# First convolution tap of three channel tiles on ScalarE instead of VectorE in a Mamba scan kernel

## The reference, cut to what matters

```python
def step(h, inp):
    d_t, B_t, C_t, u_t = inp
    h = h * jnp.exp(d_t[..., None] * A) + (d_t * u_t)[..., None] * B_t[:, None, :]
    y = jnp.einsum('bcn,bn->bc', h, C_t)
    return (h, y)
...
def _mamba_layer(x, Wi, cw, cb, Wx, Wdt, bdt, Alog, Dp, Wo):
    xz = jnp.einsum('bld,ed->ble', x, Wi)
    xin, z = jnp.split(xz, 2, axis=-1)
    xin = _silu(_causal_conv(xin, cw, cb))
    x_dbl = jnp.einsum('blc,ec->ble', xin, Wx)
    dt_raw = x_dbl[..., :DT_RANK]
    Bm = x_dbl[..., DT_RANK:DT_RANK + D_STATE]
    Cm = x_dbl[..., DT_RANK + D_STATE:]
    delta = jax.nn.softplus(jnp.einsum('blr,cr->blc', dt_raw, Wdt) + bdt)
    A = -jnp.exp(Alog)
    y = _selective_scan(delta, Bm, Cm, xin, A, Dp)
    y = y * _silu(z)
    return jnp.einsum('blc,dc->bld', y, Wo)
for i in range(DEPTH):
    x = x + _mamba_layer(x, W_in[i], conv_w[i], ...)
```

## Time and profile before

| what | value |
|---|---|
| median of 3 runs | 7742.98 us (7742.54 to 7743.24) |
| profiled execution, its own time | 7743.71 us |
| span of its trace | 7742.0 us, mean granted clock 0.987 |
| PE busy | 6941.3 us |
| DVE busy | 6668.0 us |
| ACT busy | 6422.9 us |
| POOL busy | 5929.2 us |

### The profile page before, as it was taken

The page is one execution under the profiler, slowest core; times in us unless marked ns, Lnnn a source line. Parts: engine busy times, 40 slices in busy tenths (PEclk is TensorE's granted clock), DMA queues, the critical chain, the costliest instruction groups (busy, mean ns, idle before and its releaser), DMA issues. The chain is left out here.

```text
span 7742.0 us, 143629 instructions
## 1 busy us (share of the span) xinstructions
PE 6941.3 (90%) x39999; PEld 4801.8 (62%) x39999; DVE 6668.0 (86%) x6510; ACT 6422.9 (83%) x10314; POOL 5929.2 (77%) x4917
## 2 busy tenths in 40 slices
PE   6979999999999999999999999999999999999997
PEld 4646666666666666666666666666666666666665
DVE  3259988988998899889889988988998898889888
ACT  1258888888888888888888888888888888888887
POOL 2148887888888888888888887888888788888875
PEclk9989999999999999999999999999999999999998
DMA  4111111111111111111111111111111111111112
GB/s 161 34 42 40 40 39 47 43 39 40 42 45 44 39 39 48 42 40 39 40 46 44 40 38 41 45 42 39 39 48 42 39 40 41 45 43 39 40 39 91
DMA packets 222613, 352.40 MB, mean 46 GB/s; under 512 B 43856, under 2 KB 78448, under 8 KB 221712
## 3 DMA queue, kind: packets, MB, share of 16 engines
q1 hardware_dynamic: 218048, 332.70, 14.6%
q0 software_dynamic: 3792, 10.38, 0.4%
HBM read 325.00 MB, written 17.98 MB: 44 GB/s over the span
## 5 line engine op out<-in xcount | busy, mean ns | idle before, releaser
L884 POOL TENSOR_TENSOR drive<-du,brep 128x512 f32<-128x512 f32 x4096 | 5505.9, 1374 | 708.3 <-DVE du L1127 385.6
L916 ACT ACTIVATE ps_d<-delta,cur 128x512 f32<-128x512 f32 x4096 | 2869.9, 701 | 373.9 <-DVE state L1077 354.8
L923 ACT ACTIVATE prod<-ps_r,cT 128x512 f32<-128x512 f32 x4096 | 2837.1, 693 | 245.4 <-PE ps_r L1231 243.9
L1231 PE MATMUL ps_r<-ident,state 128*128 128x128 f32 x16384 | 2564.0, 280 | 297.1 <-ACT prod L923 158.3
L1077 DVE TENSOR_TENSOR_SCAN state<-ps_d,carry,drive 128x512 f32<-128x512 f32 x2048 | 2517.7, 1266 | 260.6 <-ACT ps_d L916 258.5
L1077 DVE TENSOR_TENSOR_SCAN state<-ps_d,drive 128x512 f32<-128x512 f32 x2048 | 2396.8, 1206 | 245.6 <-ACT ps_d L916 233.0
L1238 PE MATMUL ps_y<-ident,prod 128*128 128x128 f32 x16384 | 2481.9, 276 | 25.9 <-ACT prod L923 25.9
L1238 PEld LDWEIGHTS ps_y<-ident,prod 128*128 128x128 f32 x16384 | 1938.9, 142 | 666.8 <-issue 499.4
L1231 PEld LDWEIGHTS ps_r<-ident,state 128*128 128x128 f32 x16384 | 1851.3, 142 | 729.9 <-ACT prod L923 462.5
L1278 PE MATMUL ps_r<-xm,w_inz_sb 128*128 128x512 f32 x1024 | 507.4, 618 | 81.6 <-ACT prod L923 81.6
L1270 PE MATMUL ps_r<-xm,w_inx_sb 128*128 128x512 f32 x1024 | 509.1, 620 | 21.9 <-ACT prod L923 14.2
(11 more groups left out here) (144 smaller groups left out, 4647.3 us busy)
## 6 DMA issues: line engine op xcount, KB each, us to landing
brep<-bc_dram SPq DMA_DIRECT2D x1024, 256.0 KB, 3.2
w_sb<-w SPq DMA_DIRECT2D x8, 1024.0 KB
w_all<-w SPq DMA_DIRECT2D x8, 1024.0 KB, 11.4
xb<-xs_dram SPq DMA_DIRECT2D x39, 128.5 KB, 2.0
w_all<-x SPq DMA_DIRECT2D x4, 1024.0 KB, 9.1
w_inx_sb<-w_in SPq DMA_DIRECT2D x8, 512.0 KB, 4.1
w_inz_sb<-w_in SPq DMA_DIRECT2D x8, 512.0 KB, 4.5
w_out_sb<-w_out SPq DMA_DIRECT2D x8, 512.0 KB, 4.2
```

Source lines behind the costliest of these rows:

```text
L884: nc.gpsimd.tensor_tensor(drive[:, k % DRIVE, :], du[:, j, :], brep[:, n % BREP, :], ALU.mult).then_inc(drive_set, 1)
L916: nc.scalar.activation(ps_d[:, k % 2, :], delta[h][:, j, :], ACT.Exp, scale=cur[h][:, a:a + 1]).then_inc(decay_set, 1)
L923: nc.scalar.activation(prod[:, t, :], ps_r[:, item_place(U, h, kind, item), :], ACT.Copy, scale=cT[(h + 1) % 2 if item[1] == "prev" else h ...
L1231: last = nc.tensor.transpose(out[:, j * P:(j + 1) * P], state[STATE_IN[n]][:, j, t * P:(t + 1) * P], ident[:])
```

## The change

ScalarE makes, right behind the copy of tile 0, 1 or 2, a second activation from the same place of the ring: Identity with the weight of the last tap as scale and the convolution bias as bias, written to `xc`. Only this second activation counts up `ring_act`. VectorE leaves the first tap out; its second tap now waits for that count. The two waits of tile 0 (its weights are loaded, the SiLU of the unit before has read `xc`) move to ScalarE. `conv_step` counts two instead of three steps per tile. A table `DECAYS` is introduced for the order of the exponentials; with `BOOST_AT` and `REST_AT` empty it gives the order that was there.

```diff
+BOOST_AT, REST_AT = [], []
...
+LEAD = 2
...
+DECAYS, at = {}, LEAD
+for n, j in [(n, j) for n in range(STATES) for j in range(CB)]:
+    count = 1 + BOOST_AT.count((n, j)) - REST_AT.count((n, j))
+    DECAYS[n, j] = list(range(at, at + count))
+    at += count
...
             def copy_x(U, h, kind, F, j):
+                at = item_place(U, h, kind, f"X{j}")
                 act.wait_ge(ring_ready, item_ready(U, kind, f"X{j}"))
                 act.wait_ge(halo_set, F + 1)
-                nc.scalar.activation(xpad[:, j, TAPS - 1:], ps_r[:, item_place(U, h, kind, f"X{j}"), :], ACT.Copy).then_inc(ring_act, 1)
+                copied = nc.scalar.activation(xpad[:, j, TAPS - 1:], ps_r[:, at, :], ACT.Copy)
+                if j in DVE_CONV:
+                    if j == DVE_CONV[0]:
+                        act.wait_ge(taps_in[h], loads_of(F, h))
+                        if not is_first(F):
+                            act.wait_ge(u_set, F)
+                    copied = nc.scalar.activation(xc[:, j, :], ps_r[:, at, :], ACT.Identity, scale=taps[h][:, j * TAPS + TAPS - 1:j * TAPS + TAPS],
+                                                  bias=taps[h][:, COL_CB + j:COL_CB + j + 1])
+                copied.then_inc(ring_act, 1)
...
-                if k == 0:
+                if k == 1:
                     dve.wait_ge(ring_act, copied)
-                    if j == DVE_CONV[0]:
-                        dve.wait_ge(taps_in[h], loads_of(G, h))
-                        if not is_first(G):
-                            dve.wait_ge(u_set, G)
-                    step = nc.vector.tensor_scalar(xc[:, j, :], xpad[:, j, tap:tap + T], w,
-                                                   taps[h][:, COL_CB + j:COL_CB + j + 1], ALU.mult, ALU.add)
                 else:
-                    dve.wait_ge(conv_step, (TAPS - 1) * (CV * G + DVE_CONV.index(j)) + k)
-                    step = nc.vector.scalar_tensor_tensor(xc[:, j, :], xpad[:, j, tap:tap + T], w, xc[:, j, :], ALU.mult, ALU.add)
+                    dve.wait_ge(conv_step, (TAPS - 2) * (CV * G + DVE_CONV.index(j)) + k - 1)
+                step = nc.vector.scalar_tensor_tensor(xc[:, j, :], xpad[:, j, tap:tap + T], w, xc[:, j, :], ALU.mult, ALU.add)
...
-                    if (n, j) == CONV_AT[i]:
+                    if (n, j) == CONV_AT[i] and i % TAPS:
```

More of the change, by code:

```diff
@@ L1019, in unit @@
                     for t in range(TC):
[L1020 to L1024, removed]
+                        for k in DECAYS[n, t]:
+                            if k < TILES:
+                                exponent(U, h, k)
+                            elif kind != "last":
+                                exponent(U + 1, 1 - h, k - TILES)
                         if (n, t) == SILU_AT:
@@ L1051, in _ @@
                     early(0, 0, "pre1", 1, n, t)
-            exponent(0, 0, 0)
-            exponent(0, 0, 1)
+            for k in range(LEAD):
+                exponent(0, 0, k)
             units(act, unit)
@@ L1162, in late @@
                 for i in range(CV * TAPS):
-                    if (n + STATES, j) == CONV_AT[i]:
+                    if (n + STATES, j) == CONV_AT[i] and i % TAPS:
                         conv(copied, F, hf, DVE_CONV[i // TAPS], i % TAPS)
```

## The result

The changed kernel takes **7863.15 us** (median of 4 runs, 7836.52 to 7904.57) against 7743.11 us for the kernel before beside it: ratio 1.016, 95% interval 1.0114 to 1.0205. It is slower by 120 us, outside the predicted range of 7720 to 7792. The spread is a result too: 68 us between its runs, 2 us between those of the kernel before (6 to 22 us in the larger sets of its runs beside the experiments). The profiled execution took 7871.91 us, its span is 7870.2 us.

What follows compares the result with a forecast made beforehand. No engine was saturated; the bound changes hands, mainly between VectorE and ScalarE. Activations less tap gains cost 46 us over 31 periods, the clock returns 33: +13 us, forecast 7755 us, range 7720 to 7792.

Steps and rivals of the forecast that it cites:

- Tile 0's tap in h = 1: At step (5,1), the second tap ends 0.55 us behind GpSimd's instruction, at 31.89 instead of 32.42; VectorE gains 0.52 us.
- PE's wait at `DT0`: In h = 1, PE's wait for `add_x` shrinks from 1.25 to 0.37 us, so its clock should no longer fall.
- the first rival: PE's granted clock in h = 1 keeps falling behind step (6,2), leaving only the price: 7789 us; chance 0.25.
- The price of the fall: PE's clock fall in h = 1 costs 1.07 us a period, 224.07 against 225.14 us; its absence gains 33 us.
- Scan (11,3): At tile 2, this VectorE scan waits about 0.9 us for ScalarE's exponential instead of 0.25 us.
- tile 0 with the clock: Gains at step (5,1), 0.05 us in h = 0 and 0.52 us in h = 1, plus 33 us from the clock.
- tile 1: At step (9,0), the activation costs 0.06 us in h = 0 and 0.66 us in h = 1, before scan (9,3).
- the 0.66 us in both units at tile 2: At step (11,0), the added activation is exposed in full before scan (11,3), 0.66 us in h = 0 and h = 1.
- the one on the removed tap at (15,1): Tile 2's removed VectorE tap, 0.53 us, gains at most 0.2 us before ScalarE is the bound; taken as 0.
- The rival of the passed-over tap: A second tap is held through one more GpSimd instruction once a period, 1.24 us, 38 us in all: 7793 us; chance 0.08.
- The list of edits at nothing: SiLU wait, weight loads, exponential table, GpSimd's steps, DMAs and PE's ring places were given no cost of their own.
- The third rival: VectorE is the bound: the 0.53 us at (15,1) pass on in both units, giving 7709 us; chance 0.12.

Runs made afterwards that it cites:

- tap at (15,1) put back: Changed kernel with ScalarE's loop at slot 60 and VectorE's first tap of tile 2 done once more at (15,1), same values: 7757.10 us.
- with tiles 0 and 1: Changed kernel with ScalarE's loop at slot 60 and tile 2's first tap left on VectorE as before: 7731.89 us, ratio 0.9989.
- slot 60: Changed kernel with only the start of ScalarE's loop body fixed to the 60th slot of an instruction block: 7800.87 us; the kernel before, so placed: 7745.91 us.
- tile 0 alone: Only tile 0's first tap on ScalarE, tiles 1 and 2 as in the kernel before, ScalarE's loop at slot 60: 7705.67 us, in a second set 7701.64 us.
- slot 8: The kernel before with only ScalarE's loop body moved to the eighth slot of an instruction block: 7841.71 us, ratio 1.0121.
- (1,1): Changed kernel with ScalarE's loop at slot 60 and tile 2's second tap moved from (1,0) one scan later: 7923.94 us, ratio 1.0235.
- (0,3): Changed kernel with ScalarE's loop at slot 60 and tile 2's second tap moved from (1,0) to one scan earlier: 7762.19 us, ratio 1.0027.

## Why the prediction was wrong

**What held.** The new activation takes 0.77 us (forecast about 0.78), and 0.66 us from its start to that of the next instruction, as forecast. Tile 0's tap in h = 1 ends at 3179.25, 0.55 us behind GpSimd's group, as forecast (the group below: 3167.56 + 11.14 = 3178.70), and PE's wait at `DT0` is 0.34 us (forecast 0.37). The clock in h = 1 is 1.00 behind it, against 0.79 in the earlier trace rows; in the loop it falls there in 22 of 30 units before and in none after, so the first rival is out. The price of the fall holds too: the kernel before takes 224.07 us (median) for the 7 periods in which the granted clock stays at 1.00, and 225.19 us for the 23 others. Scan (11,3) waits 0.90 us (forecast about 0.9: 0.25) and scan (9,3) waits for ScalarE.

```profile
3167.56 11.14 POOL L891 TENSOR_TENSOR drive<-du,brep 128x512 f32<-128x512 f32 x9
```

By tiles, in us:

| | forecast | measured |
|---|---|---|
| tile 0 with the clock | -18 - 33 = -51 | -39 and -43 |
| tile 1 | 31 x 0.72 = +22 | +26 to +30 |
| tile 2, tap at (15,1) put back | 31 x 1.32 = +41 | 7757.10 - 7731.89 = +25 |
| sum | +13 | 7757.10 - 7743.82 = +13 |

The terms are off by 4 to 16 us each and cancel, so the agreement of the sums is luck. The largest miss is the 0.66 us in both units at tile 2. Scan (11,3) of h = 0 and h = 1, first with tiles 0 and 1, then with all three and the tap put back (the kernel before waits 0.25 and 0.23 us):

```profile
3060.95 1.22 DVE L1104 TENSOR_TENSOR_SCAN state<-ps_d,drive 128x512 f32<-128x512 f32 x1 [0.62 <-ACT ps_d L934]
...
3173.30 1.28 DVE L1104 TENSOR_TENSOR_SCAN state<-ps_d,carry,drive 128x512 f32<-128x512 f32 x1 [0.23 <-ACT ps_d L934]
```

```profile
3070.80 1.22 DVE L1105 TENSOR_TENSOR_SCAN state<-ps_d,drive 128x512 f32<-128x512 f32 x1 [0.90 <-ACT ps_d L935]
...
3183.65 1.28 DVE L1105 TENSOR_TENSOR_SCAN state<-ps_d,carry,drive 128x512 f32<-128x512 f32 x1 [0.75 <-ACT ps_d L935]
```

Tile 1's activation had already lengthened this wait in h = 0. Tile 2's adds 0.28 and 0.52 us, and 31 x 0.80 = 25 us is what was measured. So the prices of the tiles do not simply add up.

On tile 1 the Trainium skill's rule that multiplications and additions belong on VectorE ("ScalarE: Activation LUTs", "Rules for kernel authors") is borne out, on tile 0 not: the place decides, not the operation.

**The step that failed.** Two things failed, a step and a term that was missing; the term (below) is the larger. The step is the one on the removed tap at (15,1): "The next tap after that ends with GpSimd as above, so I take 0 and keep 0.2 for the range." I asked what the removed 0.53 us were worth, and for that 0 was nearly right: at slot 60 the median period without a held tap takes 225.07 us with it removed and 225.24 us with it put back. I did not ask what the next tap would meet when it comes earlier. The rival of the passed-over tap had the mechanism, but at tile 0, with one instruction of 1.24 us a period and a chance of 0.08; the runs showed four instructions and 4.9 us at (1,0) of h = 1, in 11 of 29 units of the changed kernel and 4 of 29 in the profile at slot 60, 28 to 44 us in all.

The Trainium skill's rule ("SBUF — State Buffer", "Who interferes with whom"), that the later of the two waits until the earlier instruction is finished, would have had the tap at 3369.44 end behind the GpSimd instruction that ran when it came, so at 3369.79 + 0.54 = 3370.33. It ended at 3375.24. The earlier trace rows had already disagreed with the rule by one instruction; I gave that row too little weight.

**The term that was missing.** The list of edits at nothing names waits, the order of the exponentials, GpSimd, the DMAs and the ring. It does not name the instructions themselves: each pair of units has 8 more of them on ScalarE, and the place of the loop in memory then decides whether the jump back takes 0.4 or 2.2 to 2.6 us. That is 62 to 78 of the 120 us. No row of before shows such a stall, since ScalarE's jump was short there; but the kernel places PE's loop by hand at a slot, which was a hint that the place has a price. The trace points to a wait for instructions. Its packets of instructions show one of 8 KB that begins 0.55 to 0.97 us behind the branch where the jump is slow, and the loop's first instruction follows 1.5 to 1.9 us behind it; where the jump takes 0.4 us, that packet begins at 1.0 to 1.3 us, when the jump is over. Which engine a packet serves is not marked. The Trainium skill ("Runtime: NRT & Kernel Launch", "Instruction fetch mechanics") says that a taken branch whose target isn't in the current window of two blocks of 256 instructions has to wait for a fetch. This fits the slow jumps; but by it a loop of 764 instructions would wait wherever it lies, and the pair of runs that change nothing but the place shows that it need not. So the page alone does not explain what the place does, and how it does it stays open. Which slots are bad beyond 8 was not tried, and the trace doesn't give the slot at which the changed kernel's loop lies.

**The third rival** (VectorE is the bound) is out: at slot 60, without the tap at (15,1) and without held taps, the median period is 0.17 us shorter, not 1.06 us.

## What to carry to other kernels

When an instruction is taken away from VectorE, look at the next one that shares its time with a busy GpSimd: that it comes earlier can cost, in a period where it is held, some ten times what was taken away (4.9 us against 0.53), and a spread of the runs that jumps, here from 2 to 68 us, is the sign of it. When instructions are added in a loop, look at the time from each engine's loop-closing branch to the loop's first instruction before and after, and give the loop a fixed place if it has grown. Test a change of several like parts one by one: with the loop at slot 60, tile 0 alone is 39 to 43 us faster than the kernel before, and all three together are 56 us slower (120 us where the change left the loop).

## What the runs showed of the hardware

One of the three later taps of a tile (two operands and the result in SBUF) that meets a row of GpSimd instructions usually ends 0.55 us behind the one that was running. In some cases it is passed over by up to four more and gets its turn only when GpSimd stops, 3 to 5.8 us after it came. In h = 1 at (1,0) and (1,1), moments 0.01 to 0.03 us apart separate most of the held taps from the others, with an overlap in which both occur; that the runs differ by this is likely, but was not followed from run to run. Which moments are bad is not settled: 0.34 to 0.37 us before the end of GpSimd's instruction at (1,0), hardly at (0,3), and 0.9 and 1.03 to 1.06 us at (1,1). All held taps have in common that GpSimd runs without a pause and that the hold ends with the pause; whether fewer `drive` buffers, and so shorter rows, would limit it was not tried.

ScalarE's jump back took 0.4 us in every period at slot 60 and 2.1 to 2.6 us at slot 8, with the same 764 instructions in the loop of the kernel before. The kernels with a given slot also branch once to enter the loop, and that branch took 2.4 to 2.8 us at either slot. The profile names the idle time behind a slow jump "issue" in one kernel and a VectorE scan that had long ended in the other; only the loop's own rows show it.
